# A Mamba, cross-attention and FFN decoder layer: the first batch's start rearranged, and the diagonal B tiles built by VectorE and ScalarE instead of by DRAM

## What is computed

```python
xr = x @ W_in.T ; xc, res = xr[..., :1024], xr[..., 1024:]
u = silu(causal_depthwise_conv4(xc) + b_conv)
x_dbl = u @ W_xproj.T            # 32 columns dt, 16 columns B, 16 columns C
delta = softplus(dt @ W_dt.T + b_dt)
h_t = exp(delta_t * A) * h_{t-1} + delta_t * u_t * B_t     # 1024 channels x 16 states
y_t = sum over the 16 states of h_t * C_t  (+ u_t * D)
out = (y * silu(res)) @ W_out.T
```

## Time and profile before

| what | us |
|---|---|
| median of 3 runs | 2558.43 |
| lowest and highest of the runs | 2555.22, 2563.75 |
| the profiled execution, its own time | 2563.09 |
| its span, first to last instruction | 2561.2 |
| PE busy (share of the span) | 2349.0 (92%) |
| DVE busy | 1873.3 (73%) |
| ACT busy | 1480.3 (58%) |
| POOL busy | 1670.5 (65%) |

### The profile page before, as it was taken

How to read it: one execution, slowest core, us unless ns; L and a number is a source line. 1 busy time by engine, 2 the same in 40 slices (tenths; PEclk the granted TensorE clock), 3 DMA queues, 4 the chain that set the end, 5 groups by cost and what they waited for, 6 DMA issues and landing times. The chain is left out here.

```text
span 2561.2 us, 38124 instructions
## 1 busy us (share of the span) xinstructions
PE 2349.0 (92%) x15232; PEld 1401.8 (55%) x15232; DVE 1873.3 (73%) x2182; ACT 1480.3 (58%) x2258; POOL 1670.5 (65%) x912
## 2 busy tenths in 40 slices
PE   6799999899999999999999988777999999999997
PEld 3465566566566566566656655543445445454543
DVE  3798898998898899889889888751364565466453
ACT  3587587678678678668767757731333333443332
POOL 0698899799899889889879979860331332234130
PEclk9899999999999999999999998888999999999999
DMA  4677977877888787797787787755000000000000
GB/s 135 183 156 152 234 166 169 223 169 174 214 173 180 185 203 163 158 234 159 168 224 167 168 202 149 167 116 211 1 1 33 33 2 32 33 34 1 17 17 17
DMA packets 130384, 334.24 MB, mean 130 GB/s; under 512 B 25120, under 2 KB 73760, under 8 KB 99360
## 3 DMA queue, kind: packets, MB, share of 16 engines
q0 software_dynamic: 27648, 201.34, 39.6%
q1 hardware_dynamic: 102560, 130.46, 15.3%
HBM read 112.23 MB, written 18.20 MB: 51 GB/s over the span
## 5 line engine op out<-in xcount | busy, mean ns | idle before, releaser
L865 POOL TENSOR_TENSOR mamba_ring<-mamba_ring,mamba_c_row 128x1024 f32<-128x1024 f32 x512 | 1279.6, 2654 | 67.0 <-DVE mamba_ring L754 66.6
L754 DVE TENSOR_TENSOR_SCAN mamba_ring<-mamba_ring,ps 128x512 f32<-128x512 f32 x1024 | 1172.8, 1199 | 122.0 <-PE ps L385 119.4
L598 ACT ACTIVATE mamba_ring<-mamba_delta,mamba_a_neg 128x512 f32<-128x512 f32 x1024 | 657.6, 710 | 73.2 <-DMA mamba_ring<-mamba_ring 71.8
L385 PE MATMUL ps<-mamba_diag_b,mamba_v_t 64*128 64x128 f32 x8192 | 590.2, 287 | 86.0 <-DVE mamba_ring L754 84.6
L385 PEld LDWEIGHTS ps<-mamba_diag_b,mamba_v_t 64*128 64x128 f32 x8192 | 506.1, 191 | 278.2 <-issue 142.2
L874 POOL DMA_DIRECT2D mamba_ring<-mamba_ring x192 | 180.4, 940 | 140.0 <-DMA mamba_ring<-mamba_ring 108.8
L1521 POOL TENSOR_TENSOR xf_pr<-xf_pr,xf_top 128x1232 f32<-128x1232 f32 x32 | 75.0, 2345 | 283.7 <-DVE xf_top L1439 283.7
L298 PE MATMUL ps<-mamba_xt,mamba_wu 128*128 128x512 f32 x512 | 243.3, 621 | 17.9 <-DMA mamba_wu<-w_u 9.0
L351 PE MATMUL ps<-mamba_xt,mamba_wres 128*128 128x512 f32 x512 | 247.4, 628 | 0.0
L728 DVE SCALAR_TENSOR_TENSOR mamba_u<-ps,mamba_wcv,mamba_u 128x511 f32<-128x511 f32 (+2 forms) x192 | 142.0, 740 | 98.9 <-ACT mamba_u L561 96.3
L1514 POOL TENSOR_TENSOR xf_xn<-xf_xn,xf_bo_s 128x512 f32<-128x512 f32 x32 | 39.5, 1266 | 205.2 <-PE xf_ps L1089 205.2
(11 more groups left out here) (114 smaller groups left out, 2925.4 us busy)
## 6 DMA issues: line engine op xcount, KB each, us to landing
mamba_ring<-mamba_ring POOLq DMA_DIRECT2D x192, 1024.0 KB, 8.0
mamba_c_row<-c_rows SPq DMA_DIRECT2D x32, 1024.0 KB, 15.7
mamba_wu<-w_u SPq DMA_DIRECT2D x64, 256.0 KB, 3.9
mamba_wres<-w_res SPq DMA_DIRECT2D x64, 256.0 KB, 5.6
mamba_xt<-x_t SPq DMA_DIRECT2D x8, 1024.0 KB, 13.7
mamba_xres<-x SPq DMA_DIRECT2D x32, 256.0 KB, 8.5
x<-mamba_xres SPq DMA_DIRECT2D x32, 256.0 KB, 5.0
xf_xn<-x SPq DMA_DIRECT2D x32, 256.0 KB, 4.0
```

What stands on the lines that cost most here:

```text
L385: m = nc.tensor.matmul(ps[:, 2 * s + i, tb * P:(tb + 1) * P], v_t[g % 2][i * H:(i + 1) * H, tb * P:(tb + 1) * P], diag_b[i * H:(i + 1) * H ...
L598: a = nc.scalar.activation(ring[:, q % NR, i, :], delta[:, d % EARLY, :], ACT.Exp, scale=a_neg[:, d, 2 * k + i:2 * k + i + 1])
L754: m = nc.vector.tensor_tensor_scan(ring[:, r, i, :], ring[:, r, i, :], both[:, bass.ds(i, T, 2)], 0.0, ALU.mult, ALU.add)
L865: nc.gpsimd.tensor_tensor(ring[:, q % NR], ring[:, q % NR], c_row[:, 2 * k:2 * k + 2, :], ALU.mult).then_inc(c_done, 1)
```

## The change

- **Diagonal tiles.** The DRAM array, `blank_diag`, `store_diag`, `load_diag`, the clearing of the ring slot on POOL and ACT's wait for it are gone. `BY_DVE = (0, 3)`: DVE makes tiles 0 and 3, after the scans of k = 1 and k = 4 of block 7. `BY_ACT = (1, 2, 4, 5, 6, 7)`: ACT makes tiles 1 and 2 in block 7 at steps 2 and 3, and tiles 4, 5, 6, 7 in block 0 of the new batch at steps 0, 1, 2 and 4, behind the decays of those steps. One tile on ACT is eight instructions of 128x64.
- **Start of batch 0.** `wu` tile 0 is issued first, `x_t` in four quarters with a semaphore each, `wu` tile 1, then the four small loads; `wu` tiles 2 to 7 have buffers of their own (in ring slots that are still free), so they are issued at once, ahead of w_x, w_dt and d_skip; w_out comes last. PE starts its first product on the first quarter, and does piece j-2 of `x_product` after input product j. The softplus table is loaded ahead of `take_xdbl`. Only blocks 0 and 1 get delta ahead of the first step; `dt_pair` and `softplus` for blocks 2 and 3 are at steps (0, 2) and (0, 3) of block 0, as in the other batches. DVE makes diagonal tiles 0 to 2 ahead of the first scan and tiles 3 to 7 after the scans of k = 0 to 4 of block 0.

```diff
-    LOCAL = 4
+    BY_DVE, BY_ACT = (0, 3), (1, 2, 4, 5, 6, 7)
...
+        def wu_tile(n):
+            if 2 <= n < ND:
+                r, half = NR - 4 + n // 2 - 1, n % 2
+                return ring[:, r, half, :].rearrange("p (k q) -> p k q", k=KT)
+            return wu[n % 2]
...
-            return d if b == 0 and d < EARLY else 4 + d % 2
+            return d if b == 0 and d < 2 else 4 + d % 2
...
+            load_first_wu(0)
+            for kt in range(KT):
+                sp.dma_start(xt[0][:, kt, :], x_t[0, :, kt, :]).then_inc(xt_first[kt], 16)
+            load_first_wu(1)
             for dst, src in first_loads:
                 sp.dma_start(dst[:], src).then_inc(w_loaded, 16)
-            load_wu(0)
-            load_xt(0)
-            load_wu(1)
+            for j in range(2, ND):
+                load_first_wu(j)
...
             load_xt(1)
-            for n in range(2, ND):
-                load_wu(n)
+            sp.dma_start(wout[:], w_out).then_inc(wout_loaded, 16)
             store_c(0)
             for p in range(NC):
                 load_c(0, p)
             for n in range(ND, ND + 2):
                 load_wu(n)
-            blank_diag()
...
                     if d == ND - 1 and feeds:
                         load_c(b + 1, 0)
-                        load_diag(b + 1, 4)
...
                     if d == 5 and feeds:
                         store_c(b + 1)
-                        store_diag(b + 1)
                     if d == ND - 1 and feeds:
-                        load_diag(b + 1, 5)
-                        load_c(b + 1, 1)
-                        for k in (6, 7):
-                            load_diag(b + 1, k)
-                        for p in (2, 3):
+                        for p in range(1, NC):
                             load_c(b + 1, p)
...
-                    elif k < LOCAL:
-                        pe.wait_ge(diag_ready, NU + LOCAL * (b - 1) + k + 1)
-                    else:
-                        pe.wait_ge(diag_loaded[k], 16 * b)
+                    elif k in BY_DVE:
+                        pe.wait_ge(diag_ready, NU + len(BY_DVE) * (b - 1) + BY_DVE.index(k) + 1)
+                    elif k in BY_ACT:
+                        pe.wait_ge(diag_act, len(BY_ACT) * (b - 1) + BY_ACT.index(k) + 1)
...
             for j in range(ND):
                 u_product(j, j % 4, range(KT))
+                if j >= 2:
+                    x_product(0, [j - 2])
+            for j in (ND - 2, ND - 1):
+                x_product(0, [j])
+            pe.wait_ge(w_loaded, 16 * len(first_loads))
             pe.wait_ge(w_rest_loaded, 16 * len(rest_loads))
-            pe.wait_ge(wx_spread, 2)
-            x_product(0, range(ND))
             pe.wait_ge(xdbl_ready, 1)
-            for d in range(0, EARLY, 2):
-                dt_pair(0, d)
+            dt_pair(0, 0)
...
+            def act_diag(b, k):
+                act.wait_ge(bcol_ready, b + 1)
+                act.wait_ge(dbu_ready, (b * ND - 1) * NU + k + 1)
+                for tb in range(TT):
+                    for n in range(2):
+                        m = nc.scalar.activation(diag_b[:, tb, k, :, n], eye2[:], ACT.Copy,
+                                                 scale=b_col[:, tb, 2 * k + n:2 * k + n + 1])
+                m.then_inc(diag_act, 1)
...
-                if k == 3 and d == 0 and back:
+                if k == 3 and d == 0:
...
+                if feeds and d == 7 and k - 1 in (1, 2):
+                    act_diag(b + 1, k - 1)
+                if back and d == 0 and k in (0, 1, 2, 4):
+                    act_diag(b, (4, 5, 6, 6, 7)[k])
...
+                if g == 0 and k + AHEAD < NU:
+                    make_diag(0, k + AHEAD)
...
-                if feeds and d == 7 and k < LOCAL:
-                    make_diag(b + 1, k)
+                if feeds and d == 7 and k - 1 in BY_DVE:
+                    make_diag(b + 1, k - 1)
...
-            for k in range(NU):
+            for k in range(AHEAD):
                 make_diag(0, k)
...
-            nc.gpsimd.memset(ring[:, NR - 1], 0.0).then_inc(blanked, 1)
```

More of the change, by code:

```diff
@@ L12, with mamba_pass @@
 EPS = 1e-5
-def mamba_pass(nc, x, x_t, c_dram, diag_dram, w_u, w_res, w_conv, b_conv, w_x, w_dt, a_log, d_skip, w_out, ident_d, x1):
+def mamba_pass(nc, x, x_t, c_dram, w_u, w_res, w_conv, b_conv, w_x, w_dt, a_log, d_skip, w_out, ident_d, x1):
     NB, T, DM = x.shape
@@ L87, in mamba_pass @@
         wx_spread = sem("wx_spread")
+        wout_loaded = sem("wout_loaded")
+        xt_first = [sem(f"xt_first{kt}") for kt in range(KT)]
+        wu_first = [sem(f"wu_first{j}") for j in range(ND)]
         xt_loaded = [sem(f"xt_loaded{i}") for i in range(2)]
@@ L99, in mamba_pass @@
         diag_ready = sem("diag_ready")
[L100 to L103, removed]
+        diag_act = sem("diag_act")
         c_stored = sem("c_stored")
@@ L177, in store_c @@
                 sp.dma_start(c_dram, xdbl[C0:C0 + NS, :]).then_inc(c_stored, 16)
[L179 to L188, removed]
-                else:
[L190 to L196, removed]
-                        sp.dma_start(corners, b_col[i * H:(i + 1) * H, tb, 2 * LOCAL:NS].rearrange(
-                            "p (k n) -> p k n", n=2)).then_inc(diag_stored, 16)
[L200 to L203, removed]
-                sp.dma_start(diag_b[:, :, k].rearrange("p a t n -> p a (t n)"),
-                             diag_dram.rearrange("p (a k c) -> p a k c", a=TT, k=NU - LOCAL)[:, :, k - LOCAL, :]
-                             ).then_inc(diag_loaded[k], 16)
             def load_c(b, p):
@@ L297, in u_product @@
                 for kt in kts:
[L298 removed]
+                    if n == 0:
+                        pe.wait_ge(xt_first[kt], 16)
+                    m = nc.tensor.matmul(ps[:, bank, :], wu_tile(n)[:, kt, :], xt[b % 2][:, kt, :], start=(kt == 0),
                                          stop=(kt == KT - 1))
@@ L497, in step @@
                     dt_pair(b + 1, 0)
-                if back and (d, k) == (0, 2):
+                if (d, k) == (0, 2):
                     dt_pair(b, 2)
@@ L700, in _ @@
             silu_u(ND - 1)
+            nc.scalar.preload_act_table_set("softplus_and_others")
             take_xdbl(0)
-            for d in range(EARLY):
+            for d in range(2):
                 softplus(0, d)
```

41 lines of the change are left out of this document (22 added, 19 removed).

## The result

The changed kernel takes 2532.21 us (median of 4 runs, 2528.41 to 2542.67), the kernel before 2561.09 in the same series (4 runs, 2555.22 to 2564.28): 0.9899 of it, 95% interval 0.9867 to 0.9931. The profiled execution took 2528.41 with a span of 2526.6, 34.6 less than before. In a later series of 6 runs the same kernel took 2537.44 beside 2558.57, 0.9913 [0.9891, 0.9936]. So it is faster by 21 to 29 us; the forecast was 29, with 2529 us and a range of 2511 to 2553.

What follows compares the result with a forecast made beforehand. PE, busy 1515 of 1639 us, was taken as the bound. Start 10.5 plus DVE's part 20 minus ACT's 1.5 gave 29 us off: 2529 from the 2558.4 median (2534 for the profiled execution), range 2511 to 2553.

Steps and rivals of the forecast that it cites:

- w_x behind six wu tiles comes in time: Start of batch 0: w_x, loaded after wu tiles, would not delay x_product, which ends near 44 us.
- my rival, priced at a gain of 4 in all: Start: w_x comes late or a slow clock costs PE again; gain 4 instead of 10.5, 2535 us; chance 0.10.
- the 2.5 us that I charged for block 0: First block 0: dt_pair and softplus for blocks 2 and 3, and five make_diag between scans, give back 2.5 us.
- the bounds of 7 and 13: Start: limits around its forecast gain of 10.5 us; 7 if late w_x makes piece 0 hold up the products.
- a gain of 20: Block 7, DVE's part: 16.1 us from batches 2, 3 and 6, and 4 from batches 0, 1, 4 and 5.
- The rival of 2520: Block 7: DVE waits for one POOL instruction at most; late batches gain 9 us more, 2520; chance 0.04.
- The charge of 1.5 us: ACT's diagonal tiles: cost 1.5 us over the seven batches, bounds 0 and 14.
- The slower rival: Block 0: ACT becomes the bound at 4.0 us a tile, 49 us lost, 2577 us; chance 0.07.
- I set gain and loss to 0: Merges: coming due earlier set against landing about 0.6 us earlier each; net 0, bounds +2 a batch to block 7's gain lost.
- the first rival: Block 0: the merges give back the blocks' gain, only the start's 10.5 us remains, 2548 us; chance 0.17.
- signs that I had named for being wrong: PE waits at L385 for ACT, or at L406 for merges longer than 1.06 us; or block 0 exceeds 26.5.

Runs made afterwards that it cites:

- after_again: The changed kernel itself, unaltered, run again in a later series: 2537.44 us, 0.9913 of the kernel before.
- act_table_each: The changed kernel with one more exp table load (1.28 us) ahead of each of ACT's tiles: 2549.03 us, one run.
- all_act: The changed kernel with DVE's tiles 0 and 3 made by ACT too, so ACT makes all eight: 2535.41 us, 0.9900 of the kernel before.

## Why the prediction was right

**Start.** The first matmul came at 5.54, not 4.4; `x_product` was over at 50.03, not 44; `u_product` 8 started at 67.09, not 62.4: 8.3 ahead of before, where I had said 13. The step that failed is "w_x behind six wu tiles comes in time": it was my rival, priced at a gain of 4 in all, and it cost 3.97 and a product of 5.05 instead of 3.60, not the whole start. That wait explains 5.4 of the 6 missing at `x_product`. (The terms as I wrote them add to 39.9 for the end of product 7, not 39.0: piece 5 stands behind product 7, not ahead of it. Measured: 45.03.) Of the 2.5 us that I charged for block 0, 0.3 was paid between `u_product` 8 and block 1; all five tiles took 0.67. Net 8.0 against 10.5, inside the bounds of 7 and 13.

**Block 7, DVE's part.** I said 24.5 in three batches and 31 in four, a gain of 20. Measured 24.1 to 24.6 in three and 29.4 to 32.6 in four, a gain of 20.7: 19.9 from the three, 0.8 from the four, one of which (batch 2) lost 3.3. The mechanism held: scan 1 ahead of the tile, the tile at 0.66 if POOL is in step, the second one always at 0.66, PE's clock back at 1.00. A late tile took 3.37 to 7.50 us, not 5 to 6. Which batches are in step did not hold: 1, 3 and 6, not 2, 3 and 6. I had taken that as given, and it is the number that moves from run to run and that the later experiments moved. That it was three again, so that 20 met 20.7, is luck: the same kernel had two in step in the profile of after_again and gained 12.0 there, and its two series gave 28.9 and 21.1 us in all.

**The rule of one instruction.** By the Trainium skill (SBUF — State Buffer, Who interferes with whom) whoever issues first holds the ports for its whole instruction. The trace agrees on that, both ways: the tile at 447.12 ends at 447.79, and POOL's instruction of 447.28 takes 2.73 where its neighbour takes 2.35. What I made of it, that a waiting VectorE gets its turn behind that one instruction, did not hold: 7.50 us through four of POOL's. The rival of 2520 that rested on this is refuted.

**ACT.** 339 ns an instruction, 0.24 apart, 1.95 a tile; I had said 340, 0.25 and 2.0. It waits 0.62 and 0.31 us ahead of the two last_taps of block 0. The charge of 1.5 us was one wait of 3.43 in the last batch, where no next batch's products stand between and PE comes earlier. The slower rival needed 4.0 a tile; at 3.2 act_table_each shows how it would have gone.

**Merges.** I set gain and loss to 0. Measured: C rows land in 11.7 us at the median (15.7 before). The state sum at the end of block 0 waited 0.7 to 1.7 us for its merge in five of batches 1 to 6; now it does in two. Where it waits, the block 1 behind takes 25.3 to 25.6 us, else 24.7 (batch 4 apart), and that is the 3.3 won. Batch 4 gave 4.7 back in block 0, which is the first rival, in one batch of seven. With 3.15 of waiting for a merge, a block 0 of 31.1 and the 3.43 for ACT, signs that I had named for being wrong did show, each in a single batch.

**Sum.** For the profiled execution I had 2534; it took 2528.4, and 5.2 of the 5.6 between them lie in the stretch from the last block 7 to the end. That stretch took 874.4 us here, 878.3 in the same kernel's other profile, 879.6 before, and 875.0 to 881.2 in the rest: it is not the change. So the terms came out right to 1 us in sum, with the start 2.5 too high, the tiles 0.7 too low, and batch 7's 2.4 not in the sum: errors that cancel.

## What to carry to other kernels

A wait that shows in one instruction may be the lag of another engine that entered the stage late: take the instruction away alone, and see what is late next, before its price is booked as a gain. Where an instruction has to wait for another engine that works back to back, one longer instruction placed into a known gap did better than eight short ones. A load that nobody waits for can still hold up work, through the transfer that it stands beside.

## What the runs showed that I had not expected

- POOL keeps VectorE out across several instructions, and not the other way round: behind the first of DVE's eight 64-column instructions POOL came in at once, in five batches, while DVE stood 7.50 us through four of POOL's.
- Taking four times 1.28 us more of ACT in block 0 went with shorter blocks 7, 192.5 against 196.6 and 205.3 us in seven batches, in one profile: that a stage which runs longer lets the lagging engine catch up is my reading, and was not tried by itself. The trace speaks for it: the first merge of block 2 goes out 15.4 us after that block's first scan in every batch from 1 to 6, where the changed kernel's two profiles have up to 18.1.
- An accumulating transfer of 1 MB lands in 7.0 us beside little else, in 12.4 beside 1 MB of x and in 14.3 beside the C rows. In the changed kernel POOL stood 5.1 us for the second, in all_act PE 4.59 for the third.
